# Graph attention and gated feed forward in one launch: when the maxima of pairs 1 to 4 are formed, and one list that paces their gathers

## The chip, the cores and the metric

The kernel runs on one core of one Trainium2 chip. The metric is the device time of one launch in microseconds (us), taken as the median of several runs. Shorter is better. The core has TensorE (PE in the profile), VectorE (DVE), ScalarE (ACT), GpSimd (POOL) and the queue of SyncE (SP); they meet only through semaphores.

## The reference, cut to what matters

```python
# 6250 nodes x 256 features, 106250 edges sorted by dst, 4 heads, 8 experts
def gnn(feat, dist, W, w_src, w_dst, src, dst):
    ft = (feat @ W).reshape(n, 4, 64)
    e = sum(ft * w_src)[src] + sum(ft * w_dst)[dst]
    e = where(e >= 0, e, 0.2 * e)
    emax = segment_max(e, dst)
    ex = exp(e - emax[dst])
    a = ex / segment_sum(ex, dst)[dst] * dist
    return segment_sum(ft[src] * a, dst)
x = x + gnn(layernorm(x), ...)
h = relu(bn(einsum('bfd,edh->bfeh', layernorm(x), W1) + b1))
h = relu(bn(einsum('bfeh,ehk->bfek', h, W2) + b2))
x = x + sum over experts of (h @ Wo + bo) * softmax(router)
```

## The kernel before, in words

The 6250 nodes are 50 tiles of 125, taken as 25 pairs. A first part normalises x, projects it and writes a table of 260 columns for each node (256 features and 4 source logits). From 81.4 us on, POOL fetches for each pair the table rows of its edges: 36 indirect DMAs ("rows", line 642), 18 for each tile, into `gath`, which holds two pairs.

After that the program is a sequence of **turns**. In one turn the feed forward of pair f, the attention of pair g = f+1 and the first steps of pair a = f+2 are woven together, in 8 stages, one for each expert, and a short ninth. **T0** is the turn with f = 0 (165.4 to 236.0 us), **T1** has f = 1 (236.0 to 308.8), **T2** f = 2 (to 363.9), **T3** f = 3 (to 419.0); from T2 on every turn takes 55.1 us. Each engine has its instructions in program order, so a place in the list is also a place in time.

PE, in each stage s: layer 1 of expert s (line 791, `layer1`), layer 2 of expert s-1 (791), layer 3 of expert s-2 (820), each one block of 8 matmul records. Between them stand:
- `turn_bounds` and `to_edges` (704, 728): 36 small matmuls for pair a;
- `aggregate`: a **sum** over one quarter (chunk) of pair g's edges into `bankE`. A **whole** sum multiplies the fp32 messages directly (743). A **split** sum works on two fp32r parts, `msg_hi` (ACT, 969) and `msg_lo` (DVE, 1405), with twice the matmuls (750, 751). There is one `msg_hi` and one `msg_lo` buffer, so ACT forms the next part only after the last sum (`agg_done`). Before the change, pairs 0 to 2 use whole sums (`NATIVE = 3`), the others split ones;
- `turn_runs` and `turn_carry` (710, 711, 716): transposes for the maxima of a pair.

**The maxima of a pair** are a pass over ACT, DVE and PE: `keep_esrc` copies the fetched source logits (ACT, 958), `runs` makes two scans (DVE, 1336, 1337), `turn_runs` transposes their ends (PE), `carries` combines them over rows (DVE, 1344 to 1348), `turn_carry` transposes back, `logits` (DVE, 1375 to 1387), `exp_logits` (ACT, 974), `weigh` (DVE, 1392). Then `messages` multiplies the rows chunk by chunk (DVE, 1399). `keep_esrc` needs all rows of the pair. Steadily, the pass of pair a starts in stage 6 of its turn, two turns ahead of its feed forward. Pairs 1 and 2 are "late": their pass stands in the turn of their own sums.

`residual` (DVE, 1411 to 1425) finishes a tile from `bankE`, `root1` (ACT, 979) takes the root, `norm1` (DVE, 1429, 1431) normalises, `turn_x1` (PE, 760) and `keep_x1T` (ACT, 983) hand the pair to layer 1 of the next turn. `add_y` (DVE, 1474) adds an expert's result; PE waits for `y_added` of expert e-1 before layer 3 of expert e. `make_onehot` (DVE, 1360) makes the masks of pair a; each waits for pair g's sum of the same chunk.

A table of plans (`Plan`, `PLANS`, `STEADY`) says for each pair in which stage its steps stand. POOL waits at chosen rows for events (`pace`), so that rows spread over a turn; `BEHIND` is the steady count of rows behind each event.

Of the kernel before, what the change touches and what calls it, by code (L numbers as in the profile page):

```python
# [87 lines left out]
class Plan:  # L88


    def __init__(self, logits, sums, shift_dst, bounds, onehots, residuals, turn, runs=None, low=True):
        self.logits, self.sums, self.shift_dst, self.bounds, self.onehots = logits, sums, shift_dst, bounds, onehots
        self.residuals, self.turn, self.runs, self.low = residuals, turn, runs, low

    def messages(self, s):

        if self.low or self.runs is None:
            return self.sums.get(s + 1, ())
        first = min(self.sums) - 1
        return ((0, 1), (2, 3))[s - first] if first <= s <= first + 1 else ()  # L100
# [43 lines left out]
def gnn_ffn_kernel(nc, x, src, dst, dist, W, att_src, att_dst, Wr, br, W1, b1, g1, be1, m1, v1, W2, b2, g2, be2,  # L144
# [10 lines left out]
    with ExitStack() as ctx:  # L155
# [352 lines left out]
        def _(pool):  # L508
# [85 lines left out]
            third = released((
                (esrc_kept, 2, 2), (carry_ready, 2, 2), (h1_kept, 5, 3), (logit_ready, 2, 2), (h1_kept, 6, 2), (msg_ready, 5, 2),
                (h2_kept, 5, 1), (msg_ready, 6, 2), (msg_ready, 7, 2), (h1_kept, 7, 1), (msg_ready, 8, 2), (h2_kept, 6, 2),
                (y_added, 5, 2), (agg_done, 6, 2), (agg_done, 7, 2), (agg_done, 8, 2), (var_ready, 4, 2), (h1_kept, 8, 2),
                (xT_ready, 2, 1)))
            fourth = released(tuple(
                (sem, EX + s + d, rows) for s, counts in enumerate(((2, 1, 1), (2, 2, 1), (2, 1, 1), (2, 2, 1)))  # L600
                for (sem, d), rows in zip(((h1_kept, 1), (h2_kept, 0), (y_added, -1)), counts)) + (
                (h1_kept, 13, 2), (h2_kept, 12, 2), (y_added, 11, 2), (agg_done, 9, 2), (agg_done, 10, 2),
                (h1_kept, 14, 2), (h2_kept, 13, 2), (y_added, 12, 2), (agg_done, 11, 2)))
# [992 lines left out]
```

## Time and profile before

| what | us |
|---|---|
| median of three runs (1572.95 to 1577.39) | 1573.62 |
| the profiled execution, its device time | 1574.9 |
| the profiled span | 1573.3 |
| PE busy | 1473.4 |
| DVE busy | 1186.0 |
| POOL busy | 1073.4 |
| ACT busy | 748.8 |

The profiled execution is 1.3 us above the median, and 1.6 us of it lie outside the span. In the page's chain of work that ended last, PE has 89% of the span; lines 791 and 820 alone have 64%. An idle time in brackets is what passed on that engine just before a row, with the engine, tile and line that ended it.

### The profile page before, as it was taken

What the parts mean: (1) busy time and instruction counts of PE and PEld (TensorE: products, weight loads), DVE (VectorE), ACT (ScalarE), POOL (GpSimd) and SP (SyncE); (2) the same over time, 40 slices, a digit from 0 to 9 for tenths busy, and PEclk for the clock granted to TensorE, in tenths of its full rate; (3) what the DMA queues carried; (4) which work ended last, traced back from release to release, by engine and by line L of the source; (5) the groups of instructions that cost most, each with busy time, mean ns of one, the idle gap of its engine ahead of it and who ended that gap; (6) DMA issues with size and microseconds to landing.
All of it is one profiled execution on the core that took longest, in us unless ns stands there. A gap on an engine that the chain in (4) does not pass through costs nothing.

```text
span 1573.3 us, 23952 instructions
## 1 busy us (share of the span) xinstructions
PE 1473.4 (94%) x8358; PEld 1294.1 (82%) x8358; DVE 1186.0 (75%) x2195; ACT 748.8 (48%) x1341; POOL 1073.4 (68%) x951
## 2 busy tenths in 40 slices
PE   6904799899999999999999999999999999999998
PEld 5703588788898888888888888888888888888887
DVE  7725446588888888888888888888888888888741
ACT  3600323345545554555555455555555555555553
POOL 4175576677787778778777777877887787787000
PEclk9956899999999999999999999999999999999999
DMA  8775345434434444443444344344434434443000
GB/s 228 209 231 177 103 117 136 109 99 137 115 104 132 123 123 108 134 115 104 130 122 128 100 138 116 104 131 122 125 102 138 116 103 131 120 124 87 11 6 9
DMA packets 106070, 187.50 MB, mean 119 GB/s; under 512 B 38357, under 2 KB 70490, under 8 KB 105919
## 3 DMA queue, kind: packets, MB, share of 16 engines
q0 software_dynamic: 44688, 123.13, 28.7%
q1 hardware_dynamic: 60701, 62.29, 13.5%
q8 instruction: 68, 1.11, 0.3%
q10 hardware_dynamic: 560, 0.52, 0.1%
q14 instruction: 53, 0.43, 0.1%
HBM read 172.72 MB, written 14.42 MB: 119 GB/s over the span
## 4 chain that ended last, share of the span: by engine, by line
PE 89%; DVE 3%; POOL 3%; DMA 2%; issue 1%; ACT 1%; SPq 0%; ACTq 0%; DVEq 0%; POOLq 0%
PE bankH L791 43%; PE bankY L820 21%; PE bankE L750 7%; PE bankE L751 6%; PE bankB L728 3%; PE bankE L743 3%; POOL gath L642 3%; PE bankA L768 1%; DMA table<-gath 1%; PE bankE L670 1%; DMA gath<-table,src_win 1%; DVE gath L1399 1%; PE bankA L760 1%; PE bankE L785 1%; PE bankB L670 1%
## 5 line engine op out<-in xcount | busy, mean ns | idle before, releaser
L642 POOL DMA_INDIRECT gath<-table,src_win x900 | 1052.9, 1170 | 335.7 <-issue 249.3
L997 ACT ACTIVATE h<-bankH,bn_shift,bn_scale 128x250 f32<-128x250 f32 x800 | 401.6, 553 | 462.2 <-PE bankH L791 462.1
L791 PE MATMUL bankH<-xT,w 128*128 128x250 f32 x1600 | 378.4, 379 | 1.8 <-ACT xT L983 1.4
L820 PE MATMUL bankY<-wo,h 128*125 128x256 f32 x1600 | 378.6, 379 | 1.1 <-DVE x L1474 1.1
L791 PE MATMUL bankH<-h,w 128*128 128x250 f32 x1600 | 379.1, 379 | 0.0
L820 PEld LDWEIGHTS bankY<-wo,h 128*125 128x125 f32 x1600 | 296.3, 188 | 43.3 <-issue 1.4
L791 PEld LDWEIGHTS bankH<-h,w 128*128 128x128 f32 x1600 | 299.5, 191 | 35.7
L791 PEld LDWEIGHTS bankH<-xT,w 128*128 128x128 f32 x1600 | 296.8, 192 | 34.0 <-ACT xT L983 1.1
L1405 DVE TENSOR_TENSOR msg_lo<-gath,msg_hi 128x2340 fp32r<-128x2340 f32 x88 | 228.5, 2597 | 94.0 <-ACT msg_hi L969 94.0
L969 ACT ACTIVATE msg_hi<-gath 128x2340 fp32r<-128x2340 f32 x88 | 189.1, 2149 | 193.7 <-PE bankE L751 193.7
L1474 DVE SCALAR_TENSOR_TENSOR x<-bankY,gate,x 125x256 f32<-125x256 f32 x400 | 174.1, 477 | 120.3 <-PE bankY L820 120.0
L1399 DVE TENSOR_TENSOR gath<-gath,bankC 128x2304 f32<-128x2304 f32 x100 | 254.2, 2546 | 0.1
L750 PE MATMUL bankE<-msg_hi,onehot 128*125 128x260 f32 x792 | 205.8, 297 | 0.0
L751 PE MATMUL bankE<-msg_lo,onehot 128*125 128x260 f32 x792 | 194.3, 283 | 0.0
L750 PEld LDWEIGHTS bankE<-msg_hi,onehot 128*125 128x125 f32 x792 | 147.1, 186 | 14.5 <-issue 13.3
L751 PEld LDWEIGHTS bankE<-msg_lo,onehot 128*125 128x125 f32 x792 | 147.4, 186 | 1.2
L1360 DVE TENSOR_TENSOR onehot<-iota,bankC 128x1125 fp32r<-128x1125 f32 x100 | 130.8, 1314 | 6.4 <-PE bankE L743 6.4
L728 PE MATMUL bankB<-edst_parts,onehot_t 125*128 125x12 bf16 x900 | 59.0, 209 | 26.4 <-DVE onehot_t L1368 24.3
L728 PEld LDWEIGHTS bankB<-edst_parts,onehot_t 125*128 125x128 bf16 x900 | 59.1, 165 | 27.3 <-issue 24.4
L1368 DVE TENSOR_SCALAR onehot_t<-onehot_t,node_low 125x2304 bf16<-125x2304 bf16 x50 | 41.0, 821 | 19.1 <-DMA onehot_t<-dst_low 19.1
L743 PE MATMUL bankE<-gath,onehot 128*125 128x260 f32 x216 | 50.2, 393 | 5.1 <-DVE gath L1399 5.1
L743 PEld LDWEIGHTS bankE<-gath,onehot 128*125 128x125 f32 x216 | 41.7, 194 | 12.4 <-issue 5.2
(189 smaller groups left out, 922.8 us busy)
## 6 DMA issues: line engine op xcount, KB each, us to landing
onehot_t<-dst_low SPq DMA_DIRECT2D x48, 576.0 KB, 5.3
gath<-table,src_win POOLq DMA_INDIRECT x900, 2.9
x_res<-in_x SPq DMA_DIRECT2D x25, 250.0 KB
out<-x SPq DMA_DIRECT2D x25, 250.0 KB
table<-gath SPq DMA_DIRECT2D x25, 227.5 KB
w<-in_L_ffn_W SPq DMA_DIRECT2D x8, 512.0 KB, 10.6
gath<-in_x SPq DMA_DIRECT2D x5, 672.0 KB
wo<-in_L_ffn_Wo SPq DMA_DIRECT2D x4, 512.0 KB, 10.7
```

What stands on the lines that cost most here:

```text
L642: pool.indirect_dma_start(gath[:, g.slot(u), t, :], None, table, bass.IndirectOffsetOnAxis(src_win[:, g.win, u, t:t + 1], 0)).then_inc(row ...
L728: mm = pe.matmul(bankB[:, 0:PARTS * SEG * TE].rearrange("p (k s t) -> p k s t", k=PARTS, t=TE)[:, :, u * H:(u + 1) * H, t], onehot_t[0:NT, ...
L743: mm = pe.matmul(bankE[u][0:NT, 0:ROW], onehot[:, c, t, :].bitcast(F32), gath[:, g.slot(u), cols + t, :], start=(cols + t == 0), stop=(col ...
L750: pe.matmul(bankE[u][0:NT, 0:ROW], onehot[:, c, t, :], msg_hi[:, t, :], start=(cols + t == 0), stop=False)
L751: mm = pe.matmul(bankE[u][0:NT, 0:ROW], onehot[:, c, t, :], msg_lo[:, t, :], start=False, stop=(cols + t == TE - 1))
L791: mm = pe.matmul(target[:, hc * 2 * NT:(hc + 1) * 2 * NT], weights[:, e * KC + c, hc * P:(hc + 1) * P], operand(c), start=(c == 0), stop=( ...
L820: mm = pe.matmul(bankY[0:NT, u * D:(u + 1) * D], h2[:, e % 2, c, u, :], wo[:, e * KC + c, :], start=(c == 0), stop=(c == KC - 1))
L969: act.activation(msg_hi[:], gath[:, g.slot(c // 2), cols:cols + TC, :], ACT.Copy).then_inc(hi_ready, 1)
L997: ins = act.activation(target[:, e % 2, hc, :, :].rearrange("p u n -> p (u n)"), source[:, hc * 2 * NT:(hc + 1) * 2 * NT], ACT.Relu, bias= ...
L1399: dve.tensor_tensor(rows, rows, wgt[:, u * TE + cols:u * TE + cols + TC, :].unsqueeze(3).broadcast_to([P, TC, H, DH]), ALU.mult).then_inc( ...
L1405: dve.tensor_tensor(msg_lo[:], whole, msg_hi[:].bitcast(F32), ALU.subtract).then_inc(lo_ready, 1)
L1474: ins = dve.scalar_tensor_tensor(acc[:, u, :], bankY[0:NT, u * D:(u + 1) * D], gate[0:NT, f.par, u, e:e + 1], acc[:, u, :], ALU.mult, ALU.add)
```

## The change

The plans get more fields: `passes` says in which stage a pass of maxima begins and for which tiles (it ends one stage later), `products` in which stage each chunk's messages are made, `low` which chunks have split sums, `rush` whether the second tile is finished ahead of the masks.

- Pair 1 gets two passes in T0: tile 0 from stage 0, tile 1 from stage 2. Each pass makes the scans for both tiles, but reads new rows only for its own. Its four whole sums stand in stages 2, 3, 4 and 5, and `turn_x1` in stage 7.
- Pair 2 keeps one pass from stage 1 of T1; its sums stand in stages 3, 4, 5, 5, and chunks 1 and 2 are split.
- Pairs 3 and 4, steady before, get one pass from stage 0 of T2 and T3, with sums in stages 3 to 6, the second `residual` in stage 7 and `turn_x1` in stage 8.
- The rows of pairs 1 to 5 are released by one list of events over 180 rows, where three lists served pairs 1 to 3 and `BEHIND` the others.

```diff
-STEADY = Plan(0, dict(SOON), 1, 3, {3: (0,), 4: (1,), 5: (2,), 6: (3,)}, {5: (0,), 6: (1,)}, 7)
...
-         1: Plan(3, {5: (0,), 6: (1, 2, 3)}, 4, 5, {6: (0,), 7: (1, 2, 3)}, {7: (0, 1)}, 8, runs=2, low=False),
-         2: Plan(2, {4: (0, 1), 5: (2, 3)}, 3, 4, {5: (0, 1), 6: (2, 3)}, {5: (0,), 6: (1,)}, 7, runs=1, low=False)}
+    def __init__(self, sums, shift_dst, bounds, onehots, residuals, turn, products=None, passes=((None, (0, 1)),), low=(), rush=False):
...
+    def begins(self, s):
+        return [(k, tiles) for k, (r, tiles) in enumerate(self.passes) if r is not None and r == s]
+    def ends(self, s):
+        return self.begins(s - 1)
+USUAL = dict(shift_dst=1, bounds=3, onehots={3: (0,), 4: (1,), 5: (2,), 6: (3,)}, residuals={5: (0,), 6: (1,)})
+STEADY = Plan({2: (0,), 3: (1,), 4: (2,), 5: (3,)}, turn=7, low=ALL, **USUAL)
+         1: Plan({2: (0,), 3: (1,), 4: (2,), 5: (3,)}, 4, 5, {5: (0, 1), 6: (2, 3)}, {4: (0,), 6: (1,)}, 7,
+                 products={1: (0,), 2: (1,), 3: (2,), 4: (3,)}, passes=((0, (0,)), (2, (1,))), low=(), rush=True),
+         2: Plan({3: (0,), 4: (1,), 5: (2, 3)}, 3, 4, {4: (0,), 5: (1,), 6: (2, 3)}, {5: (0,), 6: (1,)}, 7,
+                 products={2: (0,), 3: (1,), 4: (2, 3)}, passes=((1, (0, 1)),), low=(1, 2), rush=True)}
+for n in (3, 4):
+    PLANS[n] = Plan({3: (0,), 4: (1,), 5: (2,), 6: (3,)}, 2, 3, {4: (0,), 5: (1,), 6: (2, 3)}, {5: (0,), 7: (1,)}, 8,
+                    products={2: (0,), 3: (1,), 4: (2,), 5: (3,)}, passes=((0, (0, 1)),), low=ALL)
...
+            def stage(f, behind, first=0):
+                done = (f + 1) * CHUNKS
+                for step, rows in enumerate(behind):
+                    done += len(plan_of(Pair(f + 1)).sums.get(step, ()))
+                    for sem, count, r in zip((h1_done, h2_done, y_done, agg_done),
+                                             (f * EX + step + 1, f * EX + step, f * EX + step - 1, done), rows):
+                        if r and step >= first:
+                            yield sem, count, r
...
-                (carry_ready, 1, 2), (logit_ready, 1, 2), (ex_ready, 1, 3), (msg_ready, 1, 2), (msg_ready, 2, 2), (msg_ready, 3, 2),
+                (esrc_kept, 1, 3), (carry_ready, 1, 2), (logit_ready, 1, 2), (ex_ready, 1, 3), (msg_ready, 1, 2), (msg_ready, 2, 2),
...
+            later = released((
+                *stage(0, ((0, 0, 0, 0), (0, 0, 0, 0), (1, 1, 3, 1), (1, 1, 3, 1), (1, 1, 3, 1), (3, 1, 3, 1), (1, 1, 2, 0), (1, 2, 2, 0)), 2),
+                *stage(1, ((2, 1, 2, 0), (1, 1, 2, 0), (1, 1, 2, 0), (1, 1, 3, 1), (3, 1, 2, 1), (1, 1, 4, 1), (1, 1, 2, 0), (1, 2, 2, 0))),
+                *stage(2, ((2, 1, 2, 0), (1, 1, 2, 0), (1, 1, 2, 0), (3, 1, 2, 1), (1, 1, 2, 1), (1, 2, 2, 1), (1, 1, 2, 1), (1, 2, 2, 0))),
+                *stage(3, ((2, 1, 2, 0), (1, 1, 2, 0), (1, 1, 2, 0), (3, 1, 2, 1), (1, 1, 2, 1), (1, 2, 0, 0)))))
+            DENSE = 6
+            early = [None] * 2 * TE + second + later
```

In `body` of each engine, `plan.begins(s)` issues `keep_esrc`, `runs` and `turn_runs` at the end of stage s, and `plan.ends(s)` issues `carries`, `logits`, `exp_logits`, `turn_carry` and `weigh` a stage later.

**PE, start of T0** (layer 1 of expert 0 to layer 3 of expert 0; `bankC<-ident,prefix` and `suffix` are `turn_runs`, `row_max` is `turn_carry`). Before:

```order
L768 MATMUL bankA<-wr,xT 125x8 x3
L791 MATMUL bankH<-xT,w 128x250 [waits h1_kept]
L791 MATMUL bankH<-xT,w 128x250 x3
L791 MATMUL bankH<-h,w 128x250 [waits h1_kept]
...
L820 MATMUL bankY<-wo,h 125x256 [waits h2_kept]
L820 MATMUL bankY<-wo,h 125x256 x3
L710 MATMUL bankC<-ident,prefix 8x128 [waits runs_ready]
L711 MATMUL bankC<-ident,suffix 8x128
```

Now:

```order
L804 MATMUL bankA<-wr,xT 125x8 x3
L746 MATMUL bankC<-ident,prefix 8x128 [waits runs_ready]
L747 MATMUL bankC<-ident,suffix 8x128
L827 MATMUL bankH<-xT,w 128x250 [waits h1_kept]
...
L856 MATMUL bankY<-wo,h 125x256 [waits h2_kept]
L856 MATMUL bankY<-wo,h 125x256 x3
L779 MATMUL bankE<-gath,onehot 125x260 [waits msg_ready,bias_added,onehot_ready]
L779 MATMUL bankE<-gath,onehot 125x260 x8
L746 MATMUL bankC<-ident,prefix 8x128 [waits runs_ready]
```

`turn_runs` moved ahead of layer 1 of expert 1; the first sum stands where `turn_runs` stood, and a second `turn_runs` behind it.

**DVE, end of T2** (stages 6 and 7; `onehot` is a mask of pair a, `rden` to `mv` is the second `residual`, `x<-bankY` is `add_y`, `rstd` and `xn` are `norm1`). Before:

```order
L1360 TENSOR_TENSOR onehot<-iota,bankC 128x1125 [waits agg_done]
L1336 SCALAR_TENSOR_TENSOR prefix<-reset,logit 128x152 [waits dve_step,esrc_kept]
L1337 SCALAR_TENSOR_TENSOR suffix<-reset,logit 128x152
L1411 TENSOR_SCALAR rden<-bankE 125x4 [waits x_in1,agg_done]
...
L1425 BN_AGGR mv<-stats 125x2 [waits dve_step]
L1474 SCALAR_TENSOR_TENSOR x<-bankY,gate,x 125x256 [waits y_added,y_done]
L1474 SCALAR_TENSOR_TENSOR x<-bankY,gate,x 125x256
L1429 RECIPROCAL rstd<-std 125x1 [waits std_ready]
L1431 TENSOR_SCALAR xn<-x,mv,rstd 125x256 [waits dve_step]
```

Now:

```order
L1439 TENSOR_TENSOR msg_lo<-gath,msg_hi 128x2340 [waits hi_ready]
L1394 TENSOR_TENSOR onehot<-iota,bankC 128x1125 [waits agg_done] x2
L1508 SCALAR_TENSOR_TENSOR x<-bankY,gate,x 125x256 [waits y_added,y_done]
L1508 SCALAR_TENSOR_TENSOR x<-bankY,gate,x 125x256
L1445 TENSOR_SCALAR rden<-bankE 125x4 [waits x_in1,agg_done]
...
L1459 BN_AGGR mv<-stats 125x2 [waits dve_step]
L1508 SCALAR_TENSOR_TENSOR x<-bankY,gate,x 125x256 [waits y_added,y_done]
L1508 SCALAR_TENSOR_TENSOR x<-bankY,gate,x 125x256
L1463 RECIPROCAL rstd<-std 125x1 [waits std_ready]
L1465 TENSOR_SCALAR xn<-x,mv,rstd 125x256 [waits dve_step]
```

The `add_y` between `residual` and `norm1` is that of expert 4 before and that of expert 5 now: the second `residual` moved a stage back, and the last `msg_lo` stands in stage 6.

## Rows read from the trace of the kernel before

**Rows 1.** The page, part 2: granted clock of TensorE in 40 slices.

```profile
PEclk9956899999999999999999999999999999999999
```

**Rows 2.** Stretches: length, PE, PEld, DVE, ACT, POOL busy (records), clock, DMA, GB/s.

```profile
165.40:236.00 70.60, 63.19 (x298) 53.04 (x298) 31.95 (x67) 20.38 (x43) 44.67 (x48) 0.90 0.40 110
236.00:308.70 72.70, 65.23 (x326) 55.77 (x326) 41.13 (x84) 21.68 (x46) 45.78 (x49) 0.95 0.46 124
308.70:363.80 55.10, 55.10 (x324) 48.89 (x323) 46.12 (x80) 29.30 (x48) 42.25 (x35) 1.00 0.39 103
363.80:418.90 55.10, 55.10 (x324) 48.88 (x324) 46.07 (x80) 29.30 (x48) 43.65 (x36) 1.00 0.43 120
```

**Rows 3.** Timeline of PE, T0 and start of T1: start, us, [idle before <-releaser].

```profile
163.71 1.09 PE L760 MATMUL bankA<-ident,xn 125*128 125x125 f32 x4 [4.32 <-DVE xn L1431]
165.49 3.63 PE L791 MATMUL bankH<-xT,w 128*128 128x250 f32 x8 [0.68 <-ACT xT L983]
168.95 0.94 PE L768 MATMUL bankA<-wr,xT 128*125 128x8 f32 x8
...
184.92 0.38 PE L710 MATMUL bankC<-ident,prefix 128*8 128x128 f32 x1 [5.11 <-DVE suffix L1337]
...
216.48 12.00 PE L743 MATMUL bankE<-gath,onehot 128*125 128x260 f32 x54
...
234.67 0.65 PE L760 MATMUL bankA<-ident,xn 125*128 125x125 f32 x4 [1.08 <-DVE xn L1431]
236.08 1.93 PE L791 MATMUL bankH<-xT,w 128*128 128x250 f32 x8 [0.77 <-ACT xT L983]
...
249.34 0.28 PE L710 MATMUL bankC<-ident,prefix 128*8 128x128 f32 x1 [1.72 <-DVE suffix L1337]
```

**Rows 4.** Timeline of PE, end of T1, and a split sum in T2.

```profile
300.08 0.38 PE L710 MATMUL bankC<-ident,prefix 128*8 128x128 f32 x1 [5.13 <-DVE suffix L1337]
...
343.05 0.36 PE L750 MATMUL bankE<-msg_hi,onehot 128*125 128x260 f32 x1
...
345.30 1.85 PE L791 MATMUL bankH<-xT,w 128*128 128x250 f32 x8
```

**Rows 5.** Timeline of DVE, T0 and T2.

```profile
172.55 0.19 DVE L1457 TENSOR_TENSOR gate_parts<-gate,gate_parts 125x32 fp32r<-125x32 f32 x1
...
184.02 0.47 DVE L1336 TENSOR_TENSOR_SCAN prefix<-reset,logit 128x152 f32<-128x152 f32 x1 [3.30 <-ACT logit L958]
...
340.31 2.60 DVE L1405 TENSOR_TENSOR msg_lo<-gath,msg_hi 128x2340 fp32r<-128x2340 f32 x1 [1.74 <-ACT msg_hi L969]
342.82 2.55 DVE L1399 TENSOR_TENSOR gath<-gath,bankC 128x2304 f32<-128x2304 f32 x1
...
350.26 0.15 DVE L1411 TENSOR_SCALAR rden<-bankE 125x4 f32<-125x4 f32 x1
...
352.14 1.29 DVE L1360 TENSOR_TENSOR onehot<-iota,bankC 128x1125 fp32r<-128x1125 f32 x1
...
358.78 0.86 DVE L1474 SCALAR_TENSOR_TENSOR x<-bankY,gate,x 125x256 f32<-125x256 f32 x2
359.55 0.15 DVE L1429 RECIPROCAL rstd<-std 125x1 f32<-125x1 f32 x1
```

**Rows 6.** Timeline of ACT: T0, then T2.

```profile
171.47 0.21 ACT L987 ACTIVATE rexp<-rsub 125x16 f32<-125x16 f32 x1
...
183.66 0.33 ACT L958 ACTIVATE logit<-gath 128x72 f32<-128x72 f32 x1 [4.31 <-DMA gath<-table,src_win]
...
345.56 2.15 ACT L969 ACTIVATE msg_hi<-gath 128x2340 fp32r<-128x2340 f32 x1 [3.04 <-PE bankE L751]
```

**Rows 7.** Timeline of POOL: first row of pair 1, its last, one of pair 4.

```profile
135.32 1.17 POOL L642 DMA_INDIRECT gath<-table,src_win  x1 [8.46 <-DVE row_max L1348]
...
180.89 0.95 POOL L642 DMA_INDIRECT gath<-table,src_win  x1 [0.30 <-issue]
...
322.42 2.90 POOL L642 DMA_INDIRECT gath<-table,src_win  x1 [0.30 <-PE bankH L791]
```

More of the change, by code:

```diff
@@ L88 @@
 class Plan:
[L91 to L100, printed above, removed]
@@ L114, in late, with lows, last_low, found @@
 def late(g):
-    return g is not None and plan_of(g).runs is not None
+    return g is not None and plan_of(g).passes[0][0] is not None
+def lows(g, c):
+    return sum(len(plan_of(Pair(n)).low) for n in range(g.n)) + sum(k < c for k in plan_of(g).low)
+def last_low(g, c):
+    for order in reversed(range(g.n * CHUNKS + c)):
+        if order % CHUNKS in plan_of(Pair(order // CHUNKS)).low:
+            return order + 1
+    return None
+def found(g, k):
+    return sum(len(plan_of(Pair(n)).passes) for n in range(g.n)) + k + 1
 def before(f, s, steps):
@@ L594, in _ @@
[L594 to L603, printed above, removed]
@@ L607, in pace @@
+            DENSE = 6
+            early = [None] * 2 * TE + second + later
+            assert len(second) == 2 * TE and len(early) >= DENSE * 2 * TE
             def pace(g, row):
-                if g.n in early:
-                    event = early[g.n].get(row)
+                if g.n < DENSE:
+                    event = early[g.n * 2 * TE + row]
                     if event is not None:
@@ L830, in first @@
                 turn_bounds(None, a)
-                for _ in to_edges(a):
-                    pass
-                ahead = to_edges(a + 1)
-                for _ in range(TE):
-                    next(ahead)
-                turn_runs(a)
-                turn_carry(a)
-                for _ in ahead:
-                    pass
+                for pair in (a, a + 1):
+                    for _ in to_edges(pair):
+                        pass
+                turn_runs(a, 0)
+                turn_carry(a, 0)
             def body(f, g, a):
@@ L852, in body @@
                             out_bias(f)
-                    if late(g) and s == plan.logits:
-                        turn_carry(g)
+                    for k, tiles in plan.ends(s):
+                        turn_carry(g, k)
                     if a is not None and s == plan.bounds:
@@ L866, in body @@
                         layer3(*before(f, s, 2), nothing)
-                    if late(g) and s == plan.runs:
-                        turn_runs(g)
                     if g is not None:
@@ L951, in _, with keep_esrc @@
             keep_rows(Pair(NP - 1))
-            def keep_esrc(a):
-                if not a.begins(1):
-                    act.wait_ge(logit_ready, a.n)
-                for u in range(2):
+            def keep_esrc(a, k, tiles):
+                if found(a, k) > 1:
+                    act.wait_ge(logit_ready, found(a, k) - 1)
+                for u in tiles:
                     act.wait_ge(rows_in[a.slot(u)], (a.tile(u) // SLOTS + 1) * PER_ROWS)
@@ L1044, in body @@
                         keep_gate(f)
-                    if late(g) and s == plan.runs:
-                        keep_esrc(g)
-                    if late(g) and s == plan.logits:
-                        exp_logits(g)
-                    if g is not None and plan.low:
+                    for k, tiles in plan.begins(s):
+                        keep_esrc(g, k, tiles)
+                    for k, tiles in plan.ends(s):
+                        exp_logits(g, k, tiles)
+                    if g is not None:
                         for c in plan.sums.get(s + 1, ()):
-                            keep_high(g, c)
+                            if c in plan.low:
+                                keep_high(g, c)
             def path():
@@ L1547, in body @@
                     if a is not None and not late(a) and s == 6:
[L1548 to L1549 removed]
+                        runs(a, 0)
+                    if g is not None and not plan.rush:
                         for u in plan.residuals.get(s, ()):
```

132 lines of the change are left out of this document (67 added, 65 removed).

## The prediction

> **What bounds the kernel now.** I read the granted clock by slices first: it is full everywhere except in the first part and in two places behind it [rows 1]. Then a table of stretches, one for each turn. T2 and T3 take 55.1 us each with PE busy for all of it, and so does every later turn [rows 2]: PE is the bound there, and a turn can only get longer. T0 takes 70.6 us and T1 72.7, with 7.4 and 7.5 us in which PE does nothing and a mean clock of 0.90 and 0.95 [rows 2]. So the change can win only in T0 and T1, and it also touches T2 and T3, which have nothing to give. The PE timeline says where T0 and T1 lose. In T0 PE stands 5.1 us before `turn_runs` of pair 1 [rows 3]: DVE waited for ACT, ACT 4.3 us for the last row of pair 1, issued at 180.9 [rows 5 to 7]. At the end of T0 it waits 1.1 and 0.8 us for the hand-over [rows 3]. In T1 it stands 1.7 us before `turn_runs` of pair 2 [rows 3] and 5.1 us before that of pair 3 [rows 4]. Behind a 4.3 us gap a layer block took 3.63 us; behind the short gaps of the hand-over it took 1.93 [rows 3]. A block with the clock up is 1.7 us without its drain.
>
> **The change, turn by turn.** The yardstick is 55.1 us, a turn of PE work with four split sums and no wait [rows 2]. Three whole sums took 12.0 us, 4.0 each [rows 3]; a split one took 343.05 to 345.30, 2.25 [rows 4]. So a whole sum costs 1.7 us more.
>
> *Start.* The first row of pair 1 waited for `carry_ready` [rows 7]; now it follows `esrc_kept`, 3.4 us earlier by the timeline of its neighbours, so the last row comes near 178 instead of 180.9 and tile 0's rows land before 160. The first part and pair 0's own chain are unchanged, so T0 still starts at 165.5.
>
> *T0.* Four whole sums make 55.1 + 4 x 1.7 = 61.9. The three blocks of an earlier pair are missing: -5.1. The first block runs at half clock as now: +1.7. Pair 1 has two passes: +0.6 for one more set of transposes. New: `turn_runs` comes right behind the router's matmuls, which end at 169.8, but the scans can start only after the gate parts end at 172.7 [rows 5] (`keep_esrc` is behind `rexp`, 171.7, and takes 0.33 [rows 6]). The scans take 0.85, so PE goes on at 173.6: +3.8. At the end layer 3 of expert 5 waits for `add_y` of expert 4, which is behind `norm1` and two masks: from the last sum 2.7 us to the end of ReLU 6, 1.3 table load, 0.3 root, 0.9 ReLU and 0.2 root, 0.6 `norm1`, 2.5 masks, 0.8 `add_y` = 9.3 to 9.5, against 8.95 of PE work (five blocks and `turn_x1`): +0.5. That is 63.4. The hand-over is hidden behind layer 3. The second pass is hidden behind the first whole sum: its rows are there by 184, ACT takes them at 185, the scans end near 187, the sum near 188. The unknown is the clock: 3.8 us of idle lies between the 1.7 us gap that cost nothing and the 4.3 us gap that did [rows 3]. Ends: 0 and 2.3 us (a block at 3.63 instead of 1.93, and the transposes). It is nearest the 4.3 us row, so I take 2.3. T0 = 65.7, 4.9 less than now.
>
> The Trainium skill (TensorE: Matmul & The Clock Gate, "What's actually happening") advises leaving the ramp out of a model, since it is under 1% of a typical span. This trace agrees on the size, two clock falls of some 2.3 us in 1573 us; but by that rule the sum would come out 2.3 us lower, and the whole effect here is of that order.
>
> *T1.* Two whole sums: 55.1 + 3.4 = 58.5. The wait before pair 2's `turn_runs` stays (add_y, then scans): +1.7 [rows 3]. The pass of pair 3 is gone, and with it the 5.1 us gap and the slow blocks behind it [rows 4]. What is late next is `add_y` of expert 4, as in T0: +0.5. T1 = 60.7, 12.0 less. Its two `msg_lo` are cheap in time: after a sum ACT needs 2.15 and DVE 2.5 [rows 5, 6], and PE comes to the next sum after 5.1 of blocks or more.
>
> *T2.* Pair 3's pass now begins in its own turn. `runs` is behind `add_y` of expert 6, so `turn_runs` waits as pair 2's did: +1.7. In stage 5 DVE now has a `msg_lo` 2.5, a message 2.5, a `residual` 1.9, a mask 1.2 and `add_y` 0.8 [rows 5] = 8.9 in a stage of 7.4; before, the last message stood in stage 4. A `msg_lo` that starts 2.2 us after a sum leaves PE 0.4 of slack, so the last sum comes 1.5 - 0.4 = 1.1 late. At the end the second `residual` stands in stage 7, and `norm1` behind `add_y` of expert 5, which itself waits for PE's last block. So nothing hides the hand-over: 0.8 `add_y`, 1.1 for the two `norm1`, 0.2 because the transposes have no successor, and 0.8 for the copy on ACT [rows 3, 5] = +2.9. Together 60.8, 5.7 more than now.
>
> *T3.* The same, and here pair 5 is steady, so its `runs` stands in stage 6 behind the mask of chunk 3, which waits for pair 4's last sum: 1.2 mask, 0.85 scans, 0.1 before PE's `turn_runs`: +2.2. Two sets of transposes instead of one: +0.4. T3 = 63.4, 8.3 more.
>
> *Gathers.* A row takes 0.95 and 0.3 of issue; one that meets a `msg_lo` took 2.90 [rows 7], 2.0 more (others up to 2.4). T2 must issue 41 rows and meet four `msg_lo`: 51.4 + 9 = 60.4 in 60.8 us, from about 3 us behind. Pair 4's rows are needed a turn later, and pair 5's last one is released at stage 5 of T3 and needed a stage later: hidden. If this cover were gone, the wait would show on ACT before `keep_esrc` of pair 5, up to the 4.3 us of pair 1 [rows 6]. Bounds: 0 and 5.1; I take 0. The changed window load on SP waits two messages longer for rows needed a turn later: nothing.
>
> *Sum.* T0 to T3: 65.7 + 60.7 + 60.8 + 63.4 = 250.6, against 70.6 + 72.7 + 55.1 + 55.1 = 253.5 [rows 2]. That is 2.9 us less: 1574.9 becomes 1572.0 for a profiled execution, which lies 1.3 above the median; so the median goes to 1570.7, say **1571**.
>
> **Rivals.**
>
> 1. *The clock falls at the new waits (slower).* T2 and T3 have waits of about 1.7 to 2.2 us before `turn_runs` and pairs of 2.1 and 0.8 at the hand-over. Where PE waited 1.7 us, and 1.1 and 0.8 with 0.65 of work between, the next block took 1.9 [rows 3]; where it waited 4.3, it took 3.63 [rows 3]. My waits are just above the harmless ones. If three of these five fall, each costs 2.3: +6.9, 1578. It decides from a wait of about 2 us. For it: the two hand-overs are longer than any harmless one. Against it: PE is full between them.
>
> 2. *DVE hides more than I count (much faster).* If T0's 3.8 us gap keeps the clock (2.3) and DVE delays neither last sum (2 x 1.1) nor `turn_runs` of pair 5 (2.2), the time is 6.7 lower: 1564. For it: the clock row is between two cases. Against it: the masks and scans of T3 stand in program order.
>
> 3. *The gathers become the bound.* Some rows of pair 2 or 5 come late and a stall like the 5.1 us of T0 returns, or the tile-wise passes of pair 1 wait for the same last row as now, so that the change doesn't do what it says: 1571 + 5.1 = 1576. For it: POOL has half a microsecond to spare in T2. Against it: pair 2 has 35 rows in 50 us. The Trainium skill (SBUF — State Buffer, "SBUF: two separate sides") says that VectorE and GpSimd lock a port pair against each other and the loser stands still when VectorE reads two SBUF inputs. The 2.90 us row beside a 2.60 us `msg_lo` agrees [rows 5, 7], and the change brings two such operations into T1.
>
> **How the numbers follow.** Forecast 0.45, rival 1 0.17, rival 2 0.18, rival 3 0.10, anything else 0.10. What a measurement of this kernel can tell from no change is 0.3%, 4.7 us: faster is below 1568.9, slower above 1578.3. The forecast's own range, from the clock in T0, the DVE terms and a slip of a few small waits, is 1567 to 1576. Faster: rival 2 and 0.13 of the forecast, with 0.02 of the rest, 0.33. Slower: half of rival 1, 0.02 of rival 3, and 0.08 of the rest, 0.19. Within: 0.48. The range for 8 in 10 reaches to rivals 1 and 2: 1564 to 1579.
>
> **What would show it.** In the changed profile T1 should start near 231, T2 near 292, T3 near 353 and T4 near 416 (now 419). Right: an idle time of about 4 us on PE before the first `turn_runs` of T0 and a slow block behind it; none before the second; no gap near the end of T1; waits of 2 us before `turn_x1` at the end of T2 and T3, ended by `norm1`; about 2 us before pair 5's `turn_runs`; every turn from T4 on at 55.1 us. Wrong: T2 or T3 at 56 us or less (the DVE and hand-over terms fail), blocks of 3 us in T2 or T3 (rival 1), ACT waiting on the gather DMA in T1 to T3 (rival 3), or later turns longer than 55.1.

## The result, and the profile after

| | us |
|---|---|
| kernel before, median of 20 runs (1571.86 to 1577.39) | 1573.52 |
| changed kernel, median of 20 runs (1576.43 to 1584.49) | 1580.71 |
| ratio, with its 95% interval | 1.004 [1.0031, 1.0049] |
| profiled execution of the changed kernel, device time | 1581.57 |
| its span (before 1573.3) | 1579.9 |

The change makes the kernel slower by 0.4%. The forecast was 1571, and 1580.7 lies outside its range of 1564 to 1579. The page of the changed kernel has nearly the totals of before, with 10 us more on DVE. Its clock row has one digit below 9 that [rows 1] has not, in slice 11 (395 to 434 us), the end of T3 and the start of T4:

```profile
PE 1474.8 (93%) x8362; PEld 1294.4 (82%) x8362; DVE 1196.0 (76%) x2208; ACT 753.3 (48%) x1343; POOL 1070.9 (68%) x951
...
PEclk9956899999899999999999999999999999999999
```

The table of stretches, one row for each turn from T0 to T5 (length, then PE, PEld, DVE, ACT, POOL busy, clock, DMA share, GB/s), answers to [rows 2]:

```profile
166.10:231.90 65.80, 61.79 (x302) 52.71 (x303) 38.24 (x79) 20.13 (x42) 40.59 (x43) 0.91 0.41 115
231.90:292.90 61.00, 58.67 (x324) 51.51 (x324) 41.82 (x77) 25.33 (x46) 44.38 (x43) 1.00 0.45 121
292.90:354.80 61.90, 56.20 (x324) 48.53 (x322) 48.23 (x82) 29.48 (x48) 46.10 (x43) 1.00 0.42 114
354.80:422.50 67.70, 60.16 (x326) 51.41 (x327) 49.74 (x88) 29.93 (x50) 42.78 (x39) 0.95 0.38 104
422.50:480.90 58.40, 58.40 (x322) 51.47 (x322) 44.24 (x75) 29.43 (x48) 40.32 (x33) 0.94 0.39 107
480.90:536.00 55.10, 55.10 (x324) 48.89 (x322) 46.08 (x80) 29.31 (x48) 43.67 (x36) 1.00 0.43 119
```

T0 and T1 win 4.8 and 11.8 us. T2, T3 and T4 lose 6.8, 12.6 and 3.3. T4 is the surprise: PE is busy for all of its 58.4 us and has the work of a 55.1 us turn, at a clock of 0.94. From T5 on every turn takes 55.1 us again, as before.

PE's timeline of the changed kernel (start, us, then in brackets the idle time before the row and what ended it) says where T3 and T4 lose it. The end of T2 and start of T3, the end of T3, and the start of T4:

```profile
353.37 0.65 PE L796 MATMUL bankA<-ident,xn 125*128 125x125 f32 x4 [2.13 <-DVE xn L1465]
354.79 3.42 PE L827 MATMUL bankH<-xT,w 128*128 128x250 f32 x8 [0.77 <-ACT xT L1016]
...
364.40 0.28 PE L746 MATMUL bankC<-ident,prefix 128*8 128x128 f32 x1 [1.72 <-DVE suffix L1371]
...
404.83 1.96 PE L856 MATMUL bankY<-wo,h 128*125 128x256 f32 x8 [0.55 <-DVE x L1508]
407.33 0.36 PE L786 MATMUL bankE<-msg_hi,onehot 128*125 128x260 f32 x1 [0.54 <-DVE msg_lo L1439]
...
411.90 0.28 PE L746 MATMUL bankC<-ident,prefix 128*8 128x128 f32 x1 [2.17 <-DVE suffix L1371]
...
412.12 2.61 PE L827 MATMUL bankH<-xT,w 128*128 128x250 f32 x8
414.52 2.83 PE L827 MATMUL bankH<-h,w 128*128 128x250 f32 x8
...
421.08 0.65 PE L796 MATMUL bankA<-ident,xn 125*128 125x125 f32 x4 [1.80 <-DVE xn L1465]
422.50 2.89 PE L827 MATMUL bankH<-xT,w 128*128 128x250 f32 x8 [0.77 <-ACT xT L1016]
425.18 1.69 PE L804 MATMUL bankA<-wr,xT 128*125 128x8 f32 x8
426.72 3.62 PE L827 MATMUL bankH<-h,w 128*128 128x250 f32 x8
```

Read the brackets first. Every wait that the prediction named is there, at nearly its size: 1.72 before `turn_runs`, 2.17 before that of pair 5, 2.13 and 1.80 with 0.77 at the two hand-overs. Then read the second column of the blocks behind them. Such a block takes 1.85 to 1.96 us with the clock up; here it takes 3.42, 2.61, 2.83, 2.89 and 3.62. The clock fell: the granted clock is 0.67 from 354.8 to 360.0, 0.67 from 412.1 to 417.3 and 0.56 from 422.5 to 430.2, and 1.00 from 364.4 to 404.0.

### The profile page after: what moved, and what is told of

It is laid out like the page before. It is cut to its first block, busy times and chain, and to the rows that moved or that the text cites. A ratio compares the mean times of both kernels' runs of the same rounds, so it can differ in the third digit from the quotient of the medians.

```text
span 1579.9 us, 23976 instructions
## 1 busy us (share of the span) xinstructions
PE 1474.8 (93%) x8362; PEld 1294.4 (82%) x8362; DVE 1196.0 (76%) x2208; ACT 753.3 (48%) x1343; POOL 1070.9 (68%) x951
## 4 chain that ended last, share of the span: by engine, by line
PE 88%; DVE 4%; POOL 2%; DMA 2%; issue 2%; ACT 1%; SPq 0%; DVEq 0%; ACTq 0%
PE bankH L827 43%; PE bankY L856 21%; PE bankE L786 6%; PE bankE L787 6%; PE bankB L764 3%; PE bankE L779 3%; POOL gath L678 2%; DMA table<-gath 2%; PE bankA L804 1%; PE bankA L796 1%; PE bankE L821 1%; PE bankE L706 1%; DVE x L1508 0%; DVE onehot L1394 0%; DVE gath L1433 0%
## 5 line engine op out<-in xcount | busy, mean ns | idle before, releaser
L1439 DVE TENSOR_TENSOR msg_lo<-gath,msg_hi 128x2340 fp32r<-128x2340 f32 x90 | 233.7, 2596 | 96.1 <-ACT msg_hi L1002 96.1
L1002 ACT ACTIVATE msg_hi<-gath 128x2340 fp32r<-128x2340 f32 x90 | 193.5, 2150 | 200.3 <-PE bankE L787 197.5
L786 PE MATMUL bankE<-msg_hi,onehot 128*125 128x260 f32 x810 | 210.2, 297 | 1.1 <-DVE msg_lo L1439 1.1
L787 PE MATMUL bankE<-msg_lo,onehot 128*125 128x260 f32 x810 | 198.7, 283 | 0.0
L786 PEld LDWEIGHTS bankE<-msg_hi,onehot 128*125 128x125 f32 x810 | 150.4, 186 | 16.6 <-issue 15.4
L787 PEld LDWEIGHTS bankE<-msg_lo,onehot 128*125 128x125 f32 x810 | 150.8, 186 | 1.2
L779 PE MATMUL bankE<-gath,onehot 128*125 128x260 f32 x180 | 43.8, 403 | 6.3 <-DVE gath L1433 6.3
L779 PEld LDWEIGHTS bankE<-gath,onehot 128*125 128x125 f32 x180 | 35.5, 199 | 12.9 <-issue 6.6
## 6 DMA issues: line engine op xcount, KB each, us to landing
w<-in_L_ffn_W SPq DMA_DIRECT2D x8, 512.0 KB, 11.1
```

Source lines behind the costliest of these rows:

```text
L786: pe.matmul(bankE[u][0:NT, 0:ROW], onehot[:, c, t, :], msg_hi[:, t, :], start=(cols + t == 0), stop=False)
L787: mm = pe.matmul(bankE[u][0:NT, 0:ROW], onehot[:, c, t, :], msg_lo[:, t, :], start=False, stop=(cols + t == TE - 1))
L1002: act.activation(msg_hi[:], gath[:, g.slot(c // 2), cols:cols + TC, :], ACT.Copy).then_inc(hi_ready, 1)
L1439: dve.tensor_tensor(msg_lo[:], whole, msg_hi[:].bitcast(F32), ALU.subtract).then_inc(lo_ready, 1)
```

## The experiments

Each kernel ran beside the kernel before on the same chip. The chips differ between the experiments, and the changed kernel itself was not run again beside them, so kernels are compared by their ratios to the kernel before. Theory A says that PE's granted clock falls at the waits which the change brought; theory B, that only the waits themselves cost time. The turns come from each profile's first layer block of a turn. A profile is one execution: those of e6 and g1 are the fastest of their 12 runs, that of e7 is the slowest of its 12, and that of e8 the slowest of its 6, 3.6 us above their median.

```
us                                     T0     T1     T2     T3     T4     sum
before                               70.59  72.69  55.12  55.11  55.10  308.61
changed                              65.79  60.94  61.92  67.71  58.42  314.78
e5, waits of T2 and T3 filled        66.55  60.95  61.86  64.36  55.07  308.79
e6, turn_runs a block later          65.38  60.94  60.59  65.32  55.16  307.39
e7, hand-over hidden                 65.49  60.99  60.99  64.55  53.38  305.40
e8, both                             63.72  60.46  59.31  60.70  53.36  297.55
f1, wait of T0 filled                63.88  60.94  61.82  69.45  56.61  312.70
g1, only the 0.77 us waits filled    66.68  60.95  61.88  66.02  55.09  310.62
```

In e7 and e8 one block (1.7 us) stands in the turn ahead of its own, so T2 holds 1.7 more and T4 1.7 less.

**Filling the waits (e1, e5).** The edit leaves every wait as it is and gives PE something to do in it:

```diff
+            def fill(count):
+                for _ in range(count):
+                    pe.matmul(bankE[0][:, 264:389], w1[:, 0, 0:P], w1[:, 1, 0:125], start=True, stop=True)
...
                     for k, tiles in plan.begins(s):
+                        if g.n in (3, 4):
+                            fill(7)
                         turn_runs(g, k)
...
                     if g is not None and s == plan.turn:
+                        if g.n in (3, 4):
+                            fill(8)
                         turn_x1(g)
+                        if g.n in (3, 4):
+                            fill(3)
...
+                        if a.n == 5:
+                            fill(9)
                         turn_runs(a, 0)
```

> The changed kernel, with matmuls that nobody reads (125 columns, about 0.21 us each with the clock up) put on PE into the waits that the change brought into T2 and T3: 7 before each turn_runs of pairs 3 and 4, 8 before and 3 behind each turn_x1 at the end of T2 and T3, 9 before pair 5's turn_runs. The releasers still come at the same time, so no wait gets shorter; only what PE does in it changes. Theory A (the granted clock falls at these waits, some 7 us in T2 to T4): T2 about 61.9, T3 about 64, T4 about 55.5, span about 1573, ratio to the kernel before 1.000, every block of T2 to T4 at 1.85 to 1.95. Theory B (the loss is the waits themselves, the clock is a bystander): T3 and T4 stay at 67.7 and 58.4, ratio 1.004.

The first attempt tells nothing on its question. It ran on a chip on which the kernel before took 1656.92 us (1641.85 to 1670.97); the ratio was 0.9971 [0.9942, 1.0], but T0 and T1, which it doesn't touch, have strange waits too, such as this one in T1:

```profile
254.81 0.38 PE L751 MATMUL bankC<-ident,prefix 128*8 128x128 f32 x1 [3.18 <-issue]
```

"issue" is idle time for which the profile shows no releaser; in the changed kernel's own profile this wait is 1.72 us and ended by DVE. So it was repeated on another chip.

> The kernel of the first experiment once more: its runs fell on a chip on which the kernel before took 1657 us with stretches in which PE, DVE and ACT waited for no releaser in the profile, so its turns could not be compared. Same expectations: Theory A (the clock falls at the new waits): T3 about 64, T4 about 55.5, ratio to the kernel before 1.000. Theory B (only the waits cost): T3 67.7, T4 58.4, ratio 1.004.

Measured: 1.0003 [0.999, 1.0016], against 1.004. T2, T3 and T4 run at full clock, without a layer block over 1.96 us:

```profile
295.80:357.70 61.90, 60.17 (x360) 52.95 (x358) 48.19 (x82) 29.52 (x48) 46.38 (x43) 1.00 0.41 113
357.70:422.00 64.30, 62.80 (x380) 55.23 (x381) 49.72 (x88) 29.85 (x50) 44.01 (x40) 1.00 0.41 111
422.00:477.10 55.10, 55.07 (x322) 48.90 (x322) 44.10 (x75) 29.33 (x48) 40.91 (x33) 1.00 0.41 114
```

T3 goes from 67.7 to 64.4 and T4 from 58.4 to 55.1, as theory A had it, and T2 stays. In T2 `turn_runs`, which DVE's scans release, starts 7.86 us after the turn in both kernels, and `turn_x1`, which `norm1` releases, after 60.45 us for 60.50. So theory B, which wanted 67.7 and 58.4, is refuted. The clock's share is 188.05 - 181.29 = 6.8 us over T2 to T4 in the profiles, and 0.0037 x 1574 = 5.8 us in the ratios. That is the whole difference to the kernel before.

**Norm ahead of `add_y` (e2).** DVE does `norm1` of pairs 3 and 4 before `add_y` of expert 5:

```diff
+                    soon = g is not None and g.n in (3, 4) and s == max(plan.residuals)
+                    if soon:
+                        norm1(g, 0)
+                        norm1(g, 1)
                     if run and (s >= 2 or not f.begins(1)):
                         add_y(*before(f, s, 2))
```

> The changed kernel, with norm1 of pairs 3 and 4 ahead of add_y of expert 5 on DVE at the end of T2 and T3. The 2.1 and 1.8 us waits before turn_x1 go to 0.3 or less, the 0.77 us for the copy on ACT stays. Theory A (clock): the slow blocks at the start of T3 (3.42) and T4 (2.89, 3.62) go to 1.9 with the waits, so 3.9 us of wait and about 4 of clock: about 8 less than the changed kernel, ratio to before 0.999. Theory B (only the waits count): 3.9 less, ratio 1.0015.

The same disturbed chip: 0.9964 [0.9932, 0.9996]. At the end of T2 the wait before `turn_x1` was 1.08 us, but the one behind it 4.04, and the next block took 3.67. Nothing follows for the theories from T2 to T4; the edit comes back in e7. A direct test of the wait before pair 5's `turn_runs` (e3: its scans ahead of the last mask) has no time: with that edit nothing would order DVE's read of `bankC` behind PE's write.

**`turn_runs` a block later (e6).** PE does a layer block that needs nothing from DVE before it asks for the scans:

```diff
                     for k, tiles in plan.ends(s):
-                        turn_carry(g, k)
+                        if g.n in (3, 4):
+                            turn_runs(g, k)
+                        else:
+                            turn_carry(g, k)
...
                         layer2(*before(f, s, 1), nothing)
...
+                    for k, tiles in plan.ends(s):
+                        if g.n in (3, 4):
+                            turn_carry(g, k)
```

For pair 5 `turn_runs` stands behind layer 1 of expert 7.

> The changed kernel, with turn_runs of pairs 3 and 4 one block later on PE, behind layer 1 of expert 1 (turn_carry behind layer 2 of expert 0), and turn_runs of pair 5 behind layer 1 of expert 7. The 1.7, 1.7 and 2.2 us waits before them are covered by a block of 1.85; up to 0.3 remains of the last. Both theories: -5.3 of waits. Theory A (the clock falls by the waits, so it falls less often): besides, the slow blocks at 412 to 417 (2.61, 2.83; 1.7 us) go, and perhaps those of T4: 7 to 9 less than the changed kernel, ratio to before 0.999. Theory B: 5.3 less, ratio 1.0008.

Measured: 1.0006 [0.9996, 1.0015]. The waits went as expected (1.7, 1.7, and 0.48 + 0.41 left of 2.17). The blocks of 2.61 and 2.83 are gone with them, but the start of T3 stayed slow, as nothing was changed there:

```profile
350.35 1.10 PE L796 MATMUL bankA<-ident,xn 125*128 125x125 f32 x4 [2.11 <-DVE xn L1474]
352.21 3.67 PE L827 MATMUL bankH<-xT,w 128*128 128x250 f32 x8 [0.77 <-ACT xT L1025]
...
416.12 0.65 PE L796 MATMUL bankA<-ident,xn 125*128 125x125 f32 x4 [1.55 <-DVE xn L1474]
417.53 1.93 PE L827 MATMUL bankH<-xT,w 128*128 128x250 f32 x8 [0.77 <-ACT xT L1025]
```

The two hand-overs differ by half a microsecond of wait, 2.11 against 1.55, and one block takes 3.67, the other 1.93. The ratio is theory B's 1.0008, and its interval leaves out theory A's 0.999. Theory A had counted on fewer falls. In the profile the turns sum to 7.4 us less than in the changed kernel for 4.9 us less of waits, so some clock came back there, but the start of T3 lost more than before (3.67 with 3.60 behind it). The ratio of e6 alone speaks for neither theory.

**The hand-over hidden (e7).** Norm first as in e2, both roots ahead of ReLU, and a layer block between `turn_x1` and the next turn:

```diff
                         turn_x1(g)
+                        if g.n in (3, 4):
+                            layer2(f, EX - 1, nothing)
...
-                        if f is None:
+                        if f is None or g.n in (3, 4):
                             root1(g, 1)
```

> The changed kernel, with the end of T2 and T3 arranged so that the hand-over is hidden: norm1 of pairs 3 and 4 ahead of add_y of expert 5, both roots ahead of ReLU of layer 2, and layer 2 of expert 7 between turn_x1 and layer 1 of the next turn, over the copy on ACT. The waits 2.13 + 0.77 and 1.80 + 0.77 go to 0.3 or less: -5.2. Theory A (clock): the slow blocks behind them (3.42 with its router block; 2.89, 1.69, 3.62) go as well, about 1.7 and 3.3: -10, ratio to before 0.998. Theory B: -5.2, ratio 1.001.

Measured: 0.9977 [0.9968, 0.9987], which theory B (1.001) does not reach. The waits before `turn_x1` are 0.52 and 0.45, those behind it are gone, and T3 and T4 start with blocks under 2 us. But a new fall came in T3: PE is now early at `turn_runs` of pair 4.

```profile
362.54 0.28 PE L746 MATMUL bankC<-ident,prefix 128*8 128x128 f32 x1 [2.68 <-DVE suffix L1373]
362.65 0.27 PE L747 MATMUL bankC<-ident,suffix 128*8 128x128 f32 x1
362.76 2.85 PE L827 MATMUL bankH<-xT,w 128*128 128x250 f32 x8
...
365.85 2.45 PE L827 MATMUL bankH<-h,w 128*128 128x250 f32 x8
```

**Both, and the same in T0 and T1 (e8).** `turn_runs` of pair 1's first pass and of pair 2 a block later as well.

> The edits of the last two together, and turn_runs one block later in T0 (pair 1's first) and T1 (pair 2) as well. By the terms: T0 65.8 less 1.85 of wait and the clock (1.4 to 2.3) = 62; T1 60.9 less 1.7 = 59.2; T2 61.9 less 1.7 and 2.9 = 57.3; T3 67.7 less 1.7, 2.2, 2.6 and 3.4 of clock = 57.8; T4 55.1 instead of 58.4. Sum 19 us less than the changed kernel: about 1562, ratio 0.992. Theory B, in which no clock comes back, gives 12 less: ratio 0.997. If the passes, now a block later, make the first sums late, some of it is lost again.

Measured: 0.992 [0.9906, 0.9934], a median of 1562.66 beside 1574.94: faster than both kernels, by the amount that theory A gave. The turns sum to 11.1 us less than before and 17.2 less than the changed kernel, of which 8.8 are idle time on PE (19.6 became 10.7). By turn it was not exact: T0 63.7 for 62, as its first sum now waits 1.34 us for DVE; T3 60.7 for 57.8, with 4.0 us of small waits (1.00, 0.56, 0.54, 0.48, 0.41 and 1.01) left. None of them lowers the clock:

```profile
350.90:411.60 60.70, 56.70 (x327) 48.88 (x326) 49.81 (x88) 29.98 (x50) 47.78 (x42) 1.00 0.44 120
```

**The wait of T0 filled (e4, f1).** 13 matmuls behind the router's in T0.

```diff
                         if s == 0:
                             route(f)
+                            if f.n == 0:
+                                fill(13)
```

> The changed kernel, with 13 such matmuls (2.7 us) behind the router's matmuls in the first stage of T0, inside the 3.35 us wait before pair 1's first turn_runs. The prediction priced the clock there at 2.3 us, from a block of 3.63 behind a longer wait. If that is right: T0 65.8 becomes 63.6, ratio 1.0025. If the router's slow block and the one behind the wait were at half clock for another reason (the 4.3 us wait ahead of T0), the fill gives half of it or nothing: ratio 1.0035 to 1.004.

Disturbed chip: 0.996 [0.9927, 0.9993], nothing to compare. Repeated:

> The changed kernel with 13 unread matmuls inside the first wait of T0, once more, since its first runs fell on the disturbed chip. The forecast priced the clock in T0 at 2.3 us. Theory A: the block behind the wait goes from 3.09 to 1.93 and the transposes to 0.28, T0 from 65.8 to 64.4 or less, the whole 1.5 to 2.3 less than the changed kernel, ratio to before 1.003. Theory B: nothing, 1.004.

Measured: 1.0025 [1.0015, 1.0036]. T0 went from 65.8 to 63.9, so in this pair of profiles the clock was worth 1.9 us where the forecast had 2.3. The size is loose: the same T0 took 65.4 to 66.7 in five profiles, and the interval just meets that of the changed kernel.

```profile
174.15 0.28 PE L751 MATMUL bankC<-ident,prefix 128*8 128x128 f32 x1 [0.72 <-DVE suffix L1378]
```

Its T3 is 69.45, 1.7 more than in the changed kernel with the same instructions and the same waits, and its T4 1.8 less: where and how long the clock stays down differs from one execution to the next.

**The kernel before, filled (f2).** `fill(20)` into `bankH1`, once ReLU has read it, before `turn_runs` of pair 1 in T0 and of pair 3 in T1.

```diff
                     if late(g) and s == plan.runs:
+                        if g.n == 1:
+                            pe.wait_ge(h1_kept, f.n * EX + s + 1)
+                            fill(20)
                         turn_runs(g)
```

> The kernel before, unchanged but for 20 unread matmuls (4.2 us) in each of its two 5.1 us waits: before turn_runs of pair 1 in T0 and of pair 3 in T1. No wait gets shorter. Theory A (the clock falls at waits, whatever the kernel): the blocks behind them (3.54; 3.54 and 2.67; in T0 also 2.92 and 2.63 later) go to 1.9, T0 and T1 about 2 and 2.4 us shorter, ratio 0.997. Theory B: 1.000.

Measured: 0.9983 [0.9972, 0.9994]. T0 fell from 70.6 to 67.3, and the 3.54 block behind the gap is gone. T1 did not gain (73.1 for 72.7). The blocks at its end are fast, but the clock fell at two other places, where in the first profile it held: behind 1.08 and 0.77 at the start, and in stage 3 among small matmuls.

```profile
261.04 0.38 PE L709 MATMUL bankA<-ident,bounds 128*8 128x128 f32 x2 [0.54 <-DVE bounds L1324]
263.46 3.31 PE L796 MATMUL bankH<-h,w 128*128 128x250 f32 x8
```

So the expected gain was half reached, and an expectation from one profile is no better than the clock's luck in it. The profile of f3 below has the same T0 and T1 as the kernel before, and they took 69.3 and 71.8 us there. The kernel before also has a fall in T0 without any wait just ahead of it, behind the 36 small matmuls of pair a; from 202.2 to 207.4 the granted clock is 0.67:

```profile
200.04 2.35 PE L728 MATMUL bankB<-edst_parts,onehot_t 125*128 125x12 bf16 x36
202.24 2.92 PE L791 MATMUL bankH<-h,w 128*128 128x250 f32 x8
204.96 2.63 PE L820 MATMUL bankY<-wo,h 128*125 128x256 f32 x8
```

In T0 of the changed kernel the block behind the same 36 took 1.94. So waits are not the only place at which the clock falls.

**Sixteen waits alone (f3).** The kernel before, with a wait in each of 16 full turns:

```diff
                     if run:
+                        if 6 <= f.n < 22 and s == f.n % EX:
+                            pe.wait_ge(y_added, f.n * EX + s - 2)
                         layer1(f, s, nothing)
```

> The kernel before, with one short wait put on PE in each of 16 later turns (f = 6 to 21), where before PE is never idle: ahead of layer 1 of stage f mod 8 it waits for add_y of the expert whose layer 3 it has just issued. What DVE has queued ahead of that add_y differs by stage, so the waits should range from about 1 to 4 us, two of each. The clock rises and falls with them by Theory A: behind waits up to 1.7 the next block takes 1.93, behind waits of 2.7 and more it takes 2.8 to 3.7, and between the two either may come, also for the same wait. By Theory B (no price beyond the wait) every block takes 1.93.

Measured once: 1593.2 us. 12 of the 16 made PE wait between 0.75 and 2.00 us, the others under 0.3; none reached the 2.7 us and more at which a slow block was expected. Not one lowered the clock. The longest:

```profile
960.58 1.96 PE L791 MATMUL bankH<-xT,w 128*128 128x250 f32 x8 [2.00 <-DVE x L1476]
...
1410.95 1.96 PE L791 MATMUL bankH<-xT,w 128*128 128x250 f32 x8 [1.98 <-DVE x L1476]
```

Two single waits of 2.0 us with full blocks on both sides did no harm. 2.11 to 2.13 with a second wait of 0.77 and only 0.65 us of transposes between did, in the three profiles that have it. That left the question which of the two does it.

The profiles of the disturbed chip (e1, e2, e4) answer half of it. Between 500 and 1500 us, in turns that none of the edits touches, PE stands there 31 times for a single wait of 2.08 to 2.21 us between layer 3 (with the two transposes of `turn_carry` behind it) and the next turn's layer 1. In 22 cases the next block took 1.93, in 9 it took 2.33 to 3.61. Two of them from e2:

```profile
732.37 3.61 PE L827 MATMUL bankH<-xT,w 128*128 128x250 f32 x8 [2.12 <-issue]
...
791.33 1.93 PE L827 MATMUL bankH<-xT,w 128*128 128x250 f32 x8 [2.13 <-ACT h L1030]
```

So a single wait of 2.1 us lowered the clock in some cases and left it up in others.

**Only the short wait filled (g1).** `fill(3)`, 0.6 us, behind `turn_x1` of pairs 3 and 4, and nothing else.

> The changed kernel with 3 unread matmuls (0.6 us) behind each turn_x1 of pairs 3 and 4, inside the 0.77 us wait for the copy on ACT; the waits of 2.1 and 1.8 us before turn_x1 stay empty. Waits of up to 2.0 us between full blocks never lowered the clock in the sixteen added waits, so either a wait just above 2.0 lowers it by itself, or the two waits with 0.65 us of work between them do it together. If together: the first blocks of T3 and T4 go from 3.42 and 2.89 to 1.9 or so, 3 us or more less than the changed kernel, ratio to before 1.002. If the long wait alone: the same slow blocks as before, 1.004.

Measured: 1.0015 [1.0005, 1.0025]. The long wait is as it was, and the clock holds:

```profile
351.56 0.65 PE L801 MATMUL bankA<-ident,xn 125*128 125x125 f32 x4 [2.17 <-DVE xn L1472]
352.04 0.83 PE L737 MATMUL bankE<-w 128*128 128x125 f32 x6
352.98 1.93 PE L832 MATMUL bankH<-xT,w 128*128 128x250 f32 x8
354.74 0.94 PE L809 MATMUL bankA<-wr,xT 128*125 128x8 f32 x8
```

T3 is 1.7 shorter than in the changed kernel and T4 3.3. The interval of the ratio lies clear of the changed kernel's, so this is more than one profile's luck: 0.6 us of matmuls behind each long wait gives back 3.9 of the 5.8 us that e5 gave. What the second wait adds to the first decides here, although the first can lower the clock by itself, as the 9 cases of 31 show. The blocks behind `turn_runs` of pair 5, which were left alone, are slow as before (2.80 and 2.63).

**The start of T0 filled (f4).** The kernel of e8 with `fill(18)` before `turn_x1` of pair 0 and `fill(3)` behind it, here into `bankY`.

> The eighth experiment's kernel with 18 unread matmuls ahead of turn_x1 of pair 0, in the 4.4 us wait before T0, and 3 behind it. Theory A: the transposes 1.1 to 0.65 and the first block of T0 3.70 to 1.93, 2.2 less than that kernel: ratio to before 0.9905. Theory B: 0.992, unchanged.

Measured: 0.9921 [0.9909, 0.9934], a median of 1561.74. In its profile T0 is 62.1 instead of 63.7, at full clock, and the transposes ahead of it are back to 0.65:

```profile
165.50:227.60 62.10, 58.32 (x303) 49.80 (x304) 38.18 (x79) 20.24 (x42) 42.01 (x44) 1.00 0.46 125
```

That agrees with theory A in place and size, but the ratio is that of e8: with five and six runs a difference of 2 us can't be told. The gain is not shown.

## Why the prediction was wrong

*T0 and T1: right.* 65.8 and 60.9 for 65.7 and 60.7. The first wait is 3.35 us for 3.8, the block behind it slow (3.09); the second pass of pair 1 is hidden; the 5.1 us gap at the end of T1 is gone. The clock in T0 was worth 1.9, not 2.3 (f1). That T0 comes out within 0.1 us is partly luck: the wait and the clock were each some 0.4 too high, and about as much together is missing elsewhere in the sum.

*Start:* 0.65 us late (166.14 for 165.5). It lies in the first part, which the change doesn't touch, and starts of T0 in later profiles vary from 163.5 to 168.3.

*T2: the mechanism right, 1.1 short.* Forecast 60.8, measured 61.9. The waits sum to the predicted 5.7: 61.9 less 56.2 of PE busy. PE's own work is 56.2 instead of 55.1. The five waits each cost some 0.2 us beside their idle time: the block ahead of one runs out its full 1.85, where its successor otherwise starts after 1.7, and the first block behind it takes 1.93 to 1.96 for 1.85.

*T3 and T4: the step that failed.* I forecast T3 as 55.1 plus waits and T4 as untouched: 63.4 and 55.1. They took 67.7 and 58.4. The waits were again those forecast, and with them filled (e5) T3 takes 64.4 and T4 55.1. The term that failed is the clock's cost in T2 to T4: the sum has it at nothing, and it measured 6.8 us. What stood behind the nothing were a 1.7 us wait and a pair of 1.08 and 0.77 that cost nothing in one profile [rows 3], so that waits of about 2 us were "just above the harmless ones". But whether a wait is harmless is not a matter of its length alone: the same 1.08 and 0.77 lowered the clock in f2 (3.14), and single waits of 2.1 us did so in 9 of 31 cases. The hand-over's two waits stand 0.65 us apart, and g1 shows that filling the short one keeps the clock.

I had the price and the place in rival 1: "+6.9, 1578", for three of five, at a chance of 0.17. Three of the five did fall, at both hand-overs and at pair 5's `turn_runs`. That the sum agrees is partly luck: by their slow blocks the three cost some 1.7, 3.3 and 1.7 us, not 2.3 each. The rest of the miss is small slips, all on one side: 1.1 in T2, 1.0 in T3 (64.4 in e5 for 63.4), 0.3 in T0 and T1 together, 0.65 at the start. With the 6.8 they make up the 9.6 us between 1572.0 and the profiled 1581.6, within 0.3.

The reading of the trace was short as well. It counts two clock falls behind the first part; the kernel before has four places with slow blocks there (165.5, 185.3, 202.2 and 300.5).

The Trainium skill (TensorE: Matmul & The Clock Gate, "What's actually happening") states for modelling that the ramp costs under 1% of a typical kernel's span. The size agrees here: 6.8 us in T2 to T4 and 1.9 in T0 are 0.6% of 1580. But the page does not say that a change may be priced without it, as the prediction reads it, and here it can't be: the 6.8 us are larger than the 4.7 us that a measurement can tell, and they turned no difference (1.0003) into slower (1.004).

*Rival 2* (clock kept in T0, DVE hides more) fell: the first block behind T0's wait took 3.09, and all DVE waits came. *Rival 3* (gathers) fell: ACT waited on the gather's DMA in two places for 51.3 us, both ahead of T0, and the pass of pair 5 was held by the mask and scans, not by rows:

```profile
409.77 1.33 DVE L1394 TENSOR_TENSOR onehot<-iota,bankC 128x1125 fp32r<-128x1125 f32 x1 [1.34 <-PE bankE L787]
411.01 0.47 DVE L1370 TENSOR_TENSOR_SCAN prefix<-reset,logit 128x152 f32<-128x152 f32 x1
411.39 0.45 DVE L1371 TENSOR_TENSOR_SCAN suffix<-reset,logit 128x152 f32<-128x152 f32 x1
```

*Still open.* Three waits of 0.55, 0.54 and 2.17 within 8 us lowered the clock in three profiles (changed, f1, g1) and not in those of e7 and e2. I have no rule for that, nor for how long the clock stays down. The spread of the runs says little on it: it is 8.1 us for the changed kernel (20 runs) and 4.0 for e8 (6 runs), but 6.2 for e5 (12 runs), whose waits are filled, and the start of T0 alone varies by 4.8 us.

## What to carry to other kernels

When a change brings waits of a microsecond or two to a PE that was full, put a price on the clock, too: look for waits that stand close together, and carry a slow block (1.7 us here, or two) for each such group with a chance of its own. One profile in which a wait did no harm does not make it harmless. Before pricing it, ask what PE could do in the wait: an independent block moved into it removes the wait and the risk, and even a few unread matmuls in the shorter of two neighbouring waits keep the clock. A gain taken from one turn and paid back as waits in later ones is only a gain if those are hidden: with PE's and DVE's order rearranged, the same change gives 0.992 instead of 1.004.

## What the hardware showed that I had not expected

- A 2.17 us wait followed by 0.65 of transposes and 0.83 us of unread matmuls left the clock up (block 1.93); 2.13 followed by 0.65 of transposes and 0.77 idle did not (3.42).
- The same single wait of 2.1 us between the same rows left the next block at 1.93 in 22 cases and made it 2.33 to 3.61 in 9 (e1, e2, e4).
- The fall reaches into the next turn: in T4 the router's block took 1.69 for 0.94 and layer 2 behind it 3.62 for 1.94, with no wait between.
- One of the chips ran the kernel before in 1656.92 us instead of 1574. The profiles of e1, e2 and e4, taken on it, have idle times on PE, DVE and ACT that no releaser ends.
